# Attention over sixteen heads: the products with V of two steps stand behind one another in every second step

## The reference

```
x = x + tanh(g_xattn) * attention(layernorm(x), ctx)      # 16 heads of 16, 512 queries, 512 keys, 8 batches
x = x + tanh(g_ffn)  * experts(layernorm(x))              # 8 experts, 256 -> 1024 -> 256, gated by thresholded logits
attention: q = xn Wq + bq; k, v = ctx Wk + bk, ctx Wv + bv
           p = softmax(clip(q k^T / 4)); out = (p v) Wo + bo
```

## Time and profile before

| | |
|---|---|
| median of 3 runs | 1973.48 us (1972.51 to 1974.39) |
| the profiled execution | 1972.75 us, span 1970.9 us |
| TensorE busy | 1889.1 us, 96% of the span |
| VectorE busy | 1324.8 us, 67% |
| ScalarE busy | 1243.2 us, 63% |
| mean granted clock of TensorE over the span | 0.98 of full speed |

### The profile page before, as it was taken

One profiled execution on the slowest core, in us unless ns is written; L12 is line 12 of the kernel. 1 busy time (PEld: TensorE's weight loads), 2 busy tenths in 40 slices (PEclk: granted clock), 3 DMA queues, 4 the chain that ended last, 5 costly groups with the idle time before them and its releaser, 6 DMA issues.

```text
span 1970.9 us, 25998 instructions
## 1 busy us (share of the span) xinstructions
PE 1889.1 (96%) x8916; PEld 1355.5 (69%) x8916; DVE 1324.8 (67%) x2342; ACT 1243.2 (63%) x2084; POOL 143.4 (7%) x315
## 2 busy tenths in 40 slices
PE   7889999999978999999999999999999999999998
PEld 5743333333347877788788888878878888887886
DVE  6688888888735798565655765666665566656555
ACT  4437777777753323766766766667676666667665
POOL 4300111101102260000000000000000000000000
PEclk9979999999978999999999999999999999999999
DMA  6943323222110154423324333233322224232221
GB/s 236 333 129 88 85 72 80 76 74 72 50 54 24 75 219 174 155 97 107 108 86 149 124 113 107 86 110 142 129 104 94 107 101 166 94 110 86 107 107 54
DMA packets 97243, 220.81 MB, mean 112 GB/s; under 512 B 31314, under 2 KB 49492, under 8 KB 87892
## 3 DMA queue, kind: packets, MB, share of 16 engines
q1 hardware_dynamic: 97108, 219.12, 32.3%
HBM read 178.57 MB, written 40.24 MB: 111 GB/s over the span
## 4 chain that ended last, share of the span: by engine, by line
PE 66%; DVE 2%; DMA 1%; issue 1%; ACT 1%; SPq 0%; POOL 0%; DVEq 0%; ACTq 0%; POOLq 0%
PE ps_y L2211 31%; PE ps_h L2158 27%; PE ps_h L2118 4%; PE ps_y L2130 3%; DMA blocks_scratch<-x_lo 1%; DVE h_lo L2473 0%; DVE out_T_acc L2549 0%; DVE h_hi L2469 0%; DVE gated L2542 0%; ACT gelu L2372 0%; SPq L1916 0%; DVE early L2613 0%; SPq L1925 0%; DVE candidate L2511 0%; ACT w_pair L2342 0%
## 5 line engine op out<-in xcount | busy, mean ns | idle before, releaser
L2473 DVE TENSOR_TENSOR h_lo<-gelu,h_hi 128x512 fp32r<-128x512 f32 x512 | 357.4, 702 | 406.4 <-ACT h_hi L2375 405.3
L2158 PE MATMUL ps_h<-x_hi,w_pair 128*128 128x512 f32 x1568 | 566.6, 395 | 1.3 <-ACT gelu L2372 1.0
L2372 ACT ACTIVATE gelu<-early,b 128x512 f32<-128x512 f32 x336 | 243.2, 724 | 228.8 <-DVE early L2613 222.0
L2158 PEld LDWEIGHTS ps_h<-x_hi,w_pair 128*128 128x128 f32 x1568 | 294.5, 188 | 76.9 <-issue 5.3
L978 DVE TENSOR_REDUCE low<-ps_s 128x1 f32<-128x512 f32 x512 | 322.0, 684 | 31.8 <-PE ps_s L832 28.4
L2375 ACT ACTIVATE h_hi<-gelu 128x512 fp32r<-128x512 f32 x448 | 283.3, 632 | 42.0 <-ACT gelu L2372 0.7
L2158 PE MATMUL ps_h<-x_lo,w_pair 128*128 128x512 f32 x784 | 308.7, 394 | 0.0
L1136 ACT ACTIVATE probs_T<-ps_t 128x512 f32<-128x512 f32 x384 | 207.8, 600 | 101.7 <-PE ps_t L843 100.0
L2613 DVE TENSOR_TENSOR early<-ps_h,copy 128x512 f32<-128x512 f32 x336 | 230.6, 686 | 50.6 <-PE ps_h L2158 50.5
L832 PE MATMUL ps_s<-k_st,q_st 48*128 48x512 f32 x512 | 203.4, 474 | 3.4 <-SPq L743 2.0
L2211 PE MATMUL ps_y<-h_hi,w_lo 128*128 128x512 f32 x512 | 203.0, 397 | 0.0
(11 more groups left out here) (266 smaller groups left out, 2605.2 us busy)
## 6 DMA issues: line engine op xcount, KB each, us to landing
x_hi<-blocks_scratch SPq DMA_DIRECT2D x28, 1024.0 KB, 5.1
x_lo<-blocks_scratch SPq DMA_DIRECT2D x28, 1024.0 KB, 8.8
x_hi<-blocks_scratch SPq DMA_DIRECT2D x28, 768.0 KB, 6.7
x_lo<-blocks_scratch SPq DMA_DIRECT2D x28, 768.0 KB, 10.2
gate<-gates_scratch SPq DMA_DIRECT2D x64, 256.0 KB, 3.1
q_st<-q_scratch SPq DMA_DIRECT2D x192, 64.0 KB, 2.3
k_st<-k_scratch SPq DMA_DIRECT2D x192, 64.0 KB, 2.3
k_scratch<-k_hl SPq DMA_DIRECT2D x8, 1024.0 KB, 3.9
```

Of the source, the lines that this page charges most:

```text
L2158: mm = pe.matmul(bank, w[wp], x[xp], start=start and n == 0, stop=n == 2, skip_group_check=not start)
L2372: act.activation(gelu[:, c % GELUS, :], src, ACT.Gelu_apprx_tanh, bias=b1[p][:, j:j + 1]).then_inc(gelu_done, 1)
L2473: dve.tensor_tensor(h_lo[:, j % RING, :], gelu[:, j % GELUS, :], h_hi[:, j % RING, :].bitcast(F32), ALU.subtract).then_inc(h_ready, 1)
```

## The change

In place of one PV quad (four products) in each step, every second step has two quads behind one another, and the steps between have none. In step (g, 2) stand the PV of (g, 0) and (g, 1); in step (g, 0) stand those of (2) and (3) of the group before.

```
-                        back = (b, g, k - 1) if k else (*group_after(b, g, -1), TT - 1)
+                        if k:
+                            behind = [(b, g, k - 2), (b, g, k - 1)]
+                        else:
+                            behind = [(*group_after(b, g, -1), at) for at in (TT - 2, TT - 1)]
...
-                        if exists(back[0]):
-                            probs_v(*back)
+                        if k % 2 == 0 and exists(behind[0][0]):
+                            for back in behind:
+                                probs_v(*back)
```

## The result

The changed kernel takes 2045.76 us (median of 5 runs, 2041.77 to 2050.14), the kernel before beside it 1974.39: a ratio of 1.0365, 95% interval 1.0354 to 1.0376. It is 71 us slower. The profiled execution took 2041.77 us with a span of 2039.9.

A forecast was written before the change was run, and what follows sets the result against it. The attention was taken as bound by a chain of waits through TensorE and ScalarE, no engine full; 25 us for the order plus 31 for the clock gave 56 on 1972.75, so 2028.75, put at 2029.5, range 1994 to 2052.

The forecast's parts named there:

- the forecast's own case: Whole kernel: slower, the clock falling on some of the stretches without PV, 2010 to 2045 us; chance 0.58.
- The sign and the order of pairs: Eight step pairs a batch, even PV to next: second quads cost 6.80 to 7.84, gains 4.05; attention 25 us longer.
- The second quad: Middle of each even step: the added quad costs at least 0.85 us, 0.98 if its loads hide behind nothing.
- pair 4's 0.80: Pair 4: without the odd PV, the second turn_x2, needing ScalarE's copy of the first, moves from 4.22 to 3.42.
- pair 5's 0.30: Pair 5, ending at 5.03: S of the next step waits for VectorE, putting PV at 4.73; gives 0.30.
- pairs 3, 6 and 7: The double PV ahead gives VectorE 0.85 more time, so its waits shrink: gains of 0.35, 0.89 and 0.64.
- pair 8: The plain pair, around pick_logits: 5.44 long from the third T to PV, 4.49 without the odd PV; gives 0.95.
- The odd PV ran inside waits: Pair 1: the odd PV ran inside turn_out's wait for ScalarE's low_rows, so taking it out gives 0.
- 20 x 3.8 x 0.41 = 31 us: Attention stretches without PV: 20 clock falls, mean low stay 3.8 us, each low us costing 0.41: 31 us.
- The rival in which the clock stays: Attention: T/S pairs fill the array, pauses stay short, only 22 to 30 us lost: 1995 to 2004; chance 0.25.
- Faster: Each removed PV gives its 0.98, 7.84 a batch against 6.80: 8 us faster, 1965; chance 0.05.
- copy_out's wait for PV: Sign in the profile after: ScalarE's copy_out waits 0.85 longer for PV.

The follow-up runs named there:

- The half changes: Changed kernel's move done only for PV of (g, 0), or only for PV of (g, 2), the rest as before: 2028.75 us and 2007.82 us.
- The whole filler: Changed kernel plus an unused 128 by 128 by 512 product (0.85 us of array time) in each odd step where PV stood: 2009.41 us.
- the kernel that moves only (g, 2): Kernel before, with only PV of (g, 2) moved to stand with (g, 3) in the next group's first step: 2007.82 us, ratio 1.0147.
- the half filler: Changed kernel plus an unused product of half the columns (256, 0.43 us of array time) in every odd step: 2010.95 us, ratio 1.018.
- the kernel with one quad moved: Kernel before, with only PV of (3, 2) moved to the end of step (3, 3), behind pick_logits: 1973.4 us, ratio 0.9998, 12 runs.

## Why the prediction was right, and where it was off

**The sum.** It gave 2029.5, and 2045.76 was measured: within the stated range, but 16 us above the sum and just above the 2010 to 2045 of the forecast's own case.

**The sign and the order of pairs: right, in size too.** At full clock the changed pairs add up to 59.11 a batch, 3.14 more than the earlier trace rows. If the first and the last batch lose as much, eight batches make 25 us, the value taken. That it fits so closely is partly luck: 25 was chosen for a second quad dearer than 0.85, and what fell short were the gains, 3.74 a batch in place of 4.05. Pair by pair the sums of the prediction stand against the table as 7.45, 7.86, 8.77, 6.50, 6.57, 7.33, 7.93 and 6.32: the largest miss is 0.15, in pair 6. The second quad costs 0.86, the low end of the bounds: its first loads do hide under the first quad.

**Where the gains come from: right but for pairs 4 and 5.** I had put pair 4's 0.80 and pair 5's 0.30 to the odd PV that is gone. The half changes show that 0.66 of the first and 0.26 of the second are there with that PV in place, and come from the second quad of the pair ahead, as I had said for pairs 3, 6 and 7 (0.36, 0.75 and 0.63 by the same columns). That their sizes came out near is luck. Together 2.66 of the 3.74 given back (8 x 0.86 less 3.14) are of this kind; the other 1.1 is pair 8's 0.97 and crumbs. What the runs show is that a pair behind a longer one is shorter, since an engine that was late catches up: VectorE by the waits in pairs 4 and 6 above, ScalarE in pair 5. A row of the whole execution goes with it: VectorE's reductions are idle for 64.8 us ahead of S with the clock held up, 31.8 before. No run took VectorE's work away to prove it.

```profile
L990 DVE TENSOR_REDUCE low<-ps_s 128x1 f32<-128x512 f32 x512 | 322.2, 684 | 64.8 <-PE ps_s L832 62.6
```

That row is from the page of the kernel with a filler in every odd step.

**The odd PV ran inside waits: right, and stronger than I said, but for pair 8.** turn_out stands where it stood. A filler of about PV's size in all odd steps costs 1.1 us a batch over the column of the changed kernel, 0.85 of it in pair 8.

**The clock: the right mechanism, mis-sized.** The failed term is "20 x 3.8 x 0.41 = 31 us". The price held: pairs 1, 7 and 8 are 2.83, 1.28 and 1.64 us longer than at full clock, 5.75 for 13.6 us of low clock, 0.42 per us (0.38 to 0.48 by the pair). The low time did not: I took 76 us in all. The mean granted clock is 0.9573 over the span of 2039.9 and 0.9827 over that of 1970.9 before, which is 174 and 68 us at half speed, 106 more: 13.6 in each of the six batches in the middle, 24 more in the first, 10 in the last, and 10 less behind the steps. So the term is 45, and 25 + 45 = 70; the two profiled executions differ by 69, the medians by 71. The whole filler gives about the same by another way: it takes 36 us off while it adds 1.1 a batch, 9 in all, so holding the clock was worth 45. A batch in the middle has three stays where I took 2.5, and one of them lasts 6.8 us where I took the mean of all as 3.8. The places were half wrong as well: I had listed pairs 1, 4, 5, 6 and 8. Pairs 4, 5 and 6 stay at full clock in the batches in the middle; in pair 7, which I had left out because of its gate_logits, the clock falls 1.8 us ahead of that unit, behind the wait for low_rows.

**The rival in which the clock stays** would have come out at 1974 + 25 = 1999, by the table. It is the kernel that the filler shows, less the filler's price. The Trainium skill, page "TensorE: Matmul & The Clock Gate", section "HAM oscillation — how this bites in real kernels", ties the fall to a long pause of the engine, and I gave that 0.25. The rows here don't bear it out: the longest pause ahead of a fall in the changed kernel's batches is 1.35 us, and behind the last PV before 312.7 there is none over 0.65 in the loads. In the order of before a pause of 1.30 (at 321.63) passes with the clock at 1.00. In the changed kernel itself a longer one passes too, ahead of the second turn_xn in pair 6 of every batch in the middle; the kernel that moves only (g, 2) has the same pause at the same unit, and there the clock falls, at 400.83. So the length of the pause alone does not decide it:

```profile
296.34 0.42 PEld L892 LDWEIGHTS ps_m<-ident,xn_b 128*128 128x128 f32 x4 [1.45 <-DVE x_lo L1065]
```
```profile
400.33 0.42 PEld L892 LDWEIGHTS ps_m<-ident,xn_b 128*128 128x128 f32 x4 [1.45 <-DVE x_lo L1063]
```

**Faster** would have needed gains of 6.88 a batch; they are 3.74.

**The other signs.** copy_out's wait for PV at full clock is 0.96 in step (1, 0) and 0.48 in steps (2, 0), at 285.47, and (3, 0), where there was none before; the predicted 0.85 lies between. The experts are as long as before. What stands between the third T of the last step and their first product is 3.4 us shorter (31.4 in place of 34.7), with 10 us less of low clock in it.

```profile
285.47 0.60 ACT L1145 ACTIVATE o_sb<-ps_o 128x512 f32<-128x512 f32 x1 [0.48 <-PE ps_o L854]
```

## What to carry to other kernels

Ask of each instruction that is moved whether it stands inside a wait or ahead of one: work taken out of a wait gives nothing, and put ahead of one it is paid in full, less what the engines behind it were late by anyway. When an order leaves a stretch of small products and waits, look at the granted clock before all else, since here it cost nearly twice what the order did; a product of no use in that stretch won half of the loss back. And follow a shift of some tenths of a microsecond into the next pair before you count it.

## What the hardware showed that I had not expected

The granted clock fell with only short pauses ahead of it. Around 312.7 TensorE did eight tiny pick_logits, T and S, and was busy in most of each half microsecond; those that were not are among these:

```profile
309.50:310.00 0.50, 0.29 (x4) 0.17 (x2) 0.50 (x2) 0.50 (x2) 0.31 (x1) 1.00 0.00 0
...
312.00:312.50 0.50, 0.36 (x4) 0.00 (x1) 0.50 (x1) 0.50 (x2) 0.00 (x0) 1.00 0.00 0
312.50:313.00 0.50, 0.43 (x2) 0.41 (x2) 0.50 (x2) 0.50 (x3) 0.00 (x0) 0.72 0.00 0
```

In the same batches pairs 4, 5 and 6 have turning units and waits too and keep 1.00. Batches with the same instructions at nearly the same distances can fall or not: pair 8 at 6.01 and at 7.58 above, and three of the six batches behind the first with the half filler. Such a place gives a mixture of both, and the time of the whole varies with it (1970.72 to 1982.69 over the 12 runs of the kernel with one quad moved). What decides it is left open: no run here measured it by itself.
